# Cross-attention values on four 64 by 64 parts of TensorE, copied out by ScalarE in half partitions

## The chip, the cores and the metric

The kernel runs on one core of one Trainium2 chip. The metric is the device time of one execution in microseconds (us); the time of a kernel is the median of its runs.

## What is computed

One decoder layer over x (16 batches of 64 tokens, 256 wide), in float32: self attention with 16 heads, cross attention with 16 heads over a context of 64 positions per batch, and a mixture of 16 experts with 4 per token plus a shared one. Each is added to x after a layer norm. The change lies in the cross attention:

```python
scores = jnp.einsum('bhsr,bhlr->bhsl', q_r, k_r)
attn = jax.nn.softmax(scores, axis=-1)
ctx_c = jnp.einsum('bhsl,bld->bhsd', attn, kv_r)        # the values: 64 positions l, 64 features d
ctx_lat = jnp.einsum('bhsd,hkd->bhsk', ctx_c, w_kc_kv)
ctx = ctx_lat.transpose(0, 2, 1, 3).reshape(Bv, Sv, H * K)
return ctx @ Wo.T
```

The kernel works in B = 16, S = L = 64 for these. The last two products are folded into one matrix per head before.

## The kernel before, in words

**One order for all engines.** The generators `rounds`, `middle` and `block_order` write out one list of named steps by hand. Each of the five engines walks the whole list and issues its part of each step, so on every engine the work stands in the order of the list. Semaphores alone tie the engines to each other.

**Stages.** Self attention comes first (`rounds`). Then `middle` interleaves the query rotation (`rotate`, 24 steps in two halves g of 12: twelve 128 by 128 matmuls on TensorE, L776, four products with the rope tables on VectorE, L1401, and sums on GpSimd, L1754 and L1757), the scores' left operand (`latents` and `latents_end`, matmuls on the four 64 by 64 parts of the array, L790, copied by ScalarE, L1121), and the cross attention of 8 tiles t of two batches q each. After it the router decides on experts, GpSimd scatters the rows of 8 tiles to a table in memory (`scatter`, 32 indirect transfers, L1782), and 47 blocks of 128 rows go through the experts (`block_order`).

**The cross attention of tile t** has these steps, spread out in `middle` with other work between them:
- `cross_scores`: 32 matmuls of 64 by 64 (L824) into banks 2 and 3 of PSUM. VectorE takes the row maximum off (`less_max`, L1332 and L1334, into `sm`), ScalarE takes the exponential (`cross_exp`, L1127), VectorE sums, inverts and scales (`cross_norm`, L1345, L1347, L1448, each for one head parity at a time).
- `cross_turn`: 8 records of transposes (L834); ScalarE copies them to `PX` (L1136), with partitions 64*odd + l: the head's parity `odd`, and the context position l.
- `cross_values`: for each batch q one matmul of 128 by 128 weights `kv2` by 512 columns of `PX` (L843). `kv2` is block diagonal, with the same 64 by 64 context block for both parities, so half of each product is with zeros. Float32 matmuls stand as two records each in the trace: four records a tile. Each q has a PSUM bank, which ScalarE copies to `CT` (L1144), 128 partitions by 512 elements, one copy per q.
- `cross_out`: 8 matmuls (16 records) of 128 by 256 with `CT` as weights (L852), after both copies. VectorE adds the result to x (L1453), and that frees the layer norm of the tile (`norm`, `center`, `norm_turn` with s = 2).

**What stands between.** On TensorE, between `cross_values(t)` and `cross_out(t)`: two `rotate` steps for t = 0, 1 and 2, `cross_scores(5)` for t = 3, `cross_turn(5)` for t = 4, `cross_scores(7)`, `cross_turn(6)` and a `norm_turn` for t = 5, a `norm_turn` and a `turn_hidden` for t = 6, `hidden(1)` for t = 7. On ScalarE, behind the `CT` copies: `cross_exp(2)` for t = 1; `copies(0)` (L1168) for t = 3; `expert(1)` (L1183), `copies(1)`, `cross_turn(5)`, `cross_exp(6)`, `split2` (L1161) and `split13` (L1157) for t = 4. `split2` and `split13` also have a part on GpSimd (L1765, L1761), which subtracts what ScalarE rounded.

Banks of PSUM are taken from a ring of six in these steps; `take` waits until the bank's last content is drained.

Of the kernel before, what the change touches and what calls it, by code (L numbers as in the profile page):

```python
# [8 lines left out]
ACT = mybir.ActivationFunctionType  # L9
# [298 lines left out]
def b3(t2, c):  # L308
    return t2.rearrange("p (a c) -> p a c", c=c)
# [12 lines left out]
def program(nc, x, codes, scl, woc, wos, bq, bk, bv, bo, tabs, cks, plan, empty, kvc, wqr, wkr, kckv, wot,  # L322
            wqx, kcq, wg, w13, w2, ex, out):
    with ExitStack() as ctx:
# [3 lines left out]
        def at(name, offset, shape, dt=F):  # L328
            return nc.alloc_sbuf_tensor_at(name, shape, dt, offset=offset)
# [3 lines left out]
        def keep(name, shape, dt=F):  # L333
            n = 4
            for d in shape[1:]:
                n *= d
            n = (n + 31) // 32 * 32
            t = at(name, ofs[0], shape, dt)
            ofs[0] += n
            return t  # L340
# [8 lines left out]
        kv2 = keep("kv2", [128, 16, 128])  # L349
# [117 lines left out]
        PX = at("PX", R3 + 36864, [128, 2, 8, 64])  # L467
        CT = at("CT", R3 + 40960, [128, 8, 128])
# [37 lines left out]
        ps = Banks(psum, sem)  # L506
# [72 lines left out]
        def tensor_program():  # L579
            te = Engine(nc.tensor)  # L580
            pe = nc.tensor
            ring = [0, 1, 4, 5]

            def free(b):
                if b >= 6:
                    te.wait_ge(s_x2, 8)
                te.wait_ge(ps.drained[b], ps.turn[b])
                if b in ps.lent:
                    te.wait_ge(*ps.lent.pop(b))

            def take(*name, steps=1):
                b = ring.pop(0)
                ring.append(b)
                free(b)
                return b, ps.place(b, *name, steps=steps)[0]
# [240 lines left out]
                    mm.then_inc(ps.full[b], 1)  # L836

            def cross_values(t):
                for q in range(2):
                    b, ap = take("cv", t, q)  # L840
                    te.wait_ge(*ps.emptied("ct", t, 0))
                    te.wait_ge(*ps.emptied("ct", t, 1))
                    pe.matmul(ap, kv2[:, 2 * t + q, :], PX[:, q, :, :].rearrange("p h s -> p (h s)"),  # L843
                              start=True, stop=True).then_inc(ps.full[b], 1)

            def cross_out(t):
                b, ap = take("co", t)
# [149 lines left out]
            def direct(k):  # L997
                b = NB - DIRECT + k
                ap, free = ps.place(1, "direct", k)
                if k == 0:  # L1000
# [10 lines left out]
                    "query_weights": query_weights, "rotate": rotate, "latents": latents,  # L1011
                    "latents_end": latents_end,
                    "cross_scores": cross_scores, "cross_turn": cross_turn, "cross_values": cross_values,
                    "cross_out": cross_out, "widen": widen, "logits": logits, "hidden": hidden,
                    "turn_hidden": turn_hidden, "down": down, "rank": rank, "table": table,
# [8 lines left out]
        def scalar_program():  # L1024
            sc_ = Engine(nc.scalar)
            act = nc.scalar.activation
# [110 lines left out]
                        ACT.Copy).then_inc(ps.drain("ct", t, n), 1)  # L1137

            def cross_values(t):
                for q in range(2):  # L1140
                    sc_.wait_ge(*ps.filled("cv", t, q))
                    if t > 0:
                        sc_.wait_ge(*ps.filled("co", t - 1))
                    act(CT[:, :, 64 * q:64 * q + 64], b3(ps.of("cv", t, q), 64),  # L1144
                        ACT.Copy).then_inc(ps.drain("cv", t, q), 1)

            def route(n, part):
                if part == 0:
# [68 lines left out]
            def block_down(b):  # L1217
                sc_.wait_ge(*ps.filled("by", b))
                if b >= 4:
# [5 lines left out]
                    "context_turn": context_turn, "query_key_blocks": query_key_blocks, "out_blocks": out_blocks,  # L1225
                    "query_weights": query_weights, "latents_end": latents_end, "cross_exp": cross_exp,
                    "cross_turn": cross_turn, "cross_values": cross_values, "route": route, "split13": split13,
                    "split2": split2, "copies": copies, "expert_in": expert_in, "expert": expert, "hidden": hidden,
                    "turn_hidden": turn_hidden, "block_turn": block_turn, "block_hidden": block_hidden,
# [833 lines left out]
```

## Time and profile before

| | |
|---|---|
| median of 3 runs | 550.94 us (550.25 to 551.01) |
| span of the profiled execution | 542.0 us |
| median less span | 8.9 us |
| TensorE busy | 505.6 us, 93% |
| VectorE busy | 405.6 us, 75% |
| ScalarE busy | 252.4 us, 47% |
| GpSimd busy | 200.2 us, 37% |
| chain that ended last | TensorE 67%, VectorE 18%, DMA 6%, issue 4% |
| `cross_values` on TensorE | 32 records, 288.1 to 388 us |
| `CT` copies on ScalarE | 16, median 592 ns |

Times in the profile are us from the start of the span. Busy shares are averages over stages with different limits. A row of the timeline has start, duration, engine (PE is TensorE, DVE VectorE, ACT ScalarE, POOL GpSimd), line, tile names and shapes, and in square brackets the idle time before it and what ended it. A row of the chain has start, duration and what ran; the chain is followed back from the last instruction of the kernel.

### The profile page before, as it was taken

The numbers are of one execution on the slowest core, as the hardware profiler recorded it, in microseconds if no ns is written. First come the engines' busy times: TensorE is split into PE (matmuls) and PEld (weight loads), VectorE is DVE, ScalarE is ACT, GpSimd is POOL, SyncE is SP. The second block draws the span as 40 slices with busy tenths as digits, with TensorE's granted clock in tenths as the row PEclk, the third lists the DMA queues.
The fourth block names the chain that finished last, engine by engine and source line by source line (L and its number), as shares of the span: only waits on it lengthen the run. The fifth ranks groups of instructions, "written<-read, shape, count | busy, mean of one in ns | idle before, by whom it ended". The sixth has DMA issues, their size and how long they took to land.

```text
span 542.0 us, 12555 instructions
## 1 busy us (share of the span) xinstructions
PE 505.6 (93%) x4841; PEld 412.0 (76%) x4841; DVE 405.6 (75%) x968; ACT 252.4 (47%) x560; POOL 200.2 (37%) x172
## 2 busy tenths in 40 slices
PE   5988999999999999999999999969988799999994
PEld 5767888888878889576567666747878688999993
DVE  6699875636736386999599787898886799657776
ACT  2454746537485564001212331483354687665552
POOL 7855450013100000433255244042867534544440
PEclk9899999999999999999999999997998999999998
DMA  8246100024062039993000000800282683556543
GB/s 291 112 160 197 46 2 1 1 99 186 21 211 93 2 114 372 320 346 131 1 1 2 2 1 5 309 2 14 91 268 96 212 303 99 147 164 180 168 135 118
DMA packets 22299, 68.09 MB, mean 126 GB/s; under 512 B 3979, under 2 KB 12595, under 8 KB 21204
## 3 DMA queue, kind: packets, MB, share of 16 engines
q1 hardware_dynamic: 17180, 54.45, 30.6%
q0 software_dynamic: 3600, 8.43, 4.3%
q10 hardware_dynamic: 1460, 4.40, 2.2%
q8 instruction: 40, 0.66, 0.5%
q14 instruction: 19, 0.16, 0.1%
HBM read 57.79 MB, written 28.48 MB: 159 GB/s over the span
## 4 chain that ended last, share of the span: by engine, by line
PE 67%; DVE 18%; DMA 6%; issue 4%; POOL 2%; ACT 1%; SPq 1%; POOLq 0%; DVEq 0%; ACTq 0%
PE psum L619 11%; PE psum L776 10%; PE psum L699 6%; PE psum L632 5%; PE psum L970 5%; PE psum L790 4%; PE psum L684 4%; PE psum L852 4%; DVE tt L1401 3%; DMA yv<-parts_of_tokens 3%; PE psum L652 2%; PE psum L843 2%; DVE sm L1448 2%; PE psum L661 2%; PE psum L761 2%
## 5 line engine op out<-in xcount | busy, mean ns | idle before, releaser
L1754 POOL TENSOR_TENSOR rp<-tt,tt 128x512 f32<-128x512 f32 x24 | 30.9, 1287 | 134.7 <-DVE tt L1401 134.7
L1401 DVE TENSOR_TENSOR tt<-psum,tab 128x512 f32<-128x512 f32 x96 | 60.1, 680 | 11.7 <-PE psum L776 10.7
L970 PE MATMUL psum<-EW,xgh 128*128 (+1 forms) x188 | 56.5, 343 | 1.2 <-DVE xgl L1617 1.1
L619 PE MATMUL psum<-xTh,W 128*128 128x512 f32 x128 | 52.4, 409 | 2.1 <-DVE W L1299 2.1
L1790 POOL DMA_INDIRECT parts_of_tokens<-yb,xg x35 | 35.4, 1010 | 50.1 <-ACT yb L1221 47.6
L619 PE MATMUL psum<-xTl,W 128*128 128x512 f32 x128 | 51.3, 401 | 0.0
L1363 DVE TENSOR_TENSOR OTl<-psum,OTh 128x256 fp32r<-128x256 f32 (+1 forms) x49 | 23.2, 502 | 26.9 <-ACT OTh L1084 26.8
L776 PE MATMUL psum<-xTh,Ah 128*128 128x512 f32 x96 | 40.1, 418 | 0.0
L1782 POOL DMA_INDIRECT rows_of_experts<-xe,posi x32 | 33.7, 1052 | 14.0 <-issue 8.6
L776 PE MATMUL psum<-xTh,Al 128*128 128x512 f32 x96 | 38.0, 396 | 0.0
L776 PE MATMUL psum<-xTl,Ah 128*128 128x512 f32 x96 | 38.0, 396 | 0.0
L970 PEld LDWEIGHTS psum<-EW,xgh 128*128 128x128 f32 x188 | 34.1, 188 | 2.1 <-issue 1.9
L699 PE MATMUL psum<-wo,OTh 128*128 128x256 f32 x128 | 34.1, 300 | 0.0
L1617 DVE TENSOR_TENSOR xgl<-psum,xgh 128x256 fp32r<-128x256 f32 x47 | 19.7, 422 | 18.5 <-ACT xgh L1203 18.1
L1121 ACT ACTIVATE qP<-psum 128x512 f32<-128x512 f32 x16 | 8.7, 595 | 51.4 <-PE psum L790 51.4
L1696 POOL TENSOR_TENSOR rst<-bst,half 128x1 f32<-128x1 f32 x24 | 13.0, 553 | 50.9 <-DVE bst L1258 50.2
L699 PE MATMUL psum<-wo,OTl 128*128 128x256 f32 x128 | 31.7, 282 | 0.0
L790 PE MATMUL psum<-rp,Mb 64*64 64x512 f32 x256 | 30.8, 599 | 0.8 <-DVE rp L1426 0.6
L1048 ACT ACTIVATE qT<-psum,bqs 128x512 f32<-128x512 f32 x32 | 21.9, 685 | 20.3 <-PE psum L619 20.2
L852 PE MATMUL psum<-Fb,CT 128*128 128x256 f32 x128 | 30.6, 394 | 0.2 <-ACT CT L1144 0.2
L619 PEld LDWEIGHTS psum<-xTh,W 128*128 128x128 f32 x128 | 24.6, 192 | 8.0 <-DVE W L1299 2.3
L970 PE MATMUL psum<-EW,xgl 128*128 (+1 forms) x94 | 30.4, 323 | 0.0
(263 smaller groups left out, 1462.0 us busy)
## 6 DMA issues: line engine op xcount, KB each, us to landing
rows_of_experts<-in_empty SPq DMA_DIRECT2D x8, 2064.0 KB, 24.7
exr<-in_ex SPq DMA_DIRECT2D x9, 608.0 KB, 6.8
xg<-rows_of_experts SPq DMA_DIRECT2D x39, 129.0 KB, 2.2
exr<-in_ex ACTq DMA_DIRECT2D x7, 608.0 KB, 6.3
yv<-parts_of_tokens SPq DMA_DIRECT2D x8, 512.0 KB, 4.3
raw<-in_codes SPq DMA_DIRECT2D x6, 512.0 KB, 6.4
raw<-in_codes SPq DMA_DIRECT2D x3, 1024.0 KB, 8.0
wor<-in_woc SPq DMA_DIRECT2D x4, 512.0 KB, 3.8
```

What stands on the lines that cost most here:

```text
L619: mm = pe.matmul(ap, W[:, kt, m, 512 * hq + 128 * h:512 * hq + 128 * h + 128], xp[:, kt, 512 * g:512 * g + 512], start=(n == 0), stop=(n = ...
L632: mm = pe.matmul(ap, xp[:, kt, 128 * t:128 * t + 128], W[:, kt, 2, 512 * hq:512 * hq + 512], start=(n == 0), stop=(n == 3))
L699: mm = pe.matmul(dst, part[i % 2][:, 128 * h:128 * h + 128], wo[:, 4 * hq + h, :], start=(hq == 0 and h == 0 and n == 0 and i % 2 == 0), s ...
L776: mm = pe.matmul(ap, w[:, kt, half_, 128 * j:128 * j + 128], xp[:, kt, 512 * g:512 * g + 512], start=(n == 0), stop=(n == 5))
L790: mm = pe.matmul(ps.of(*name)[64 * side:64 * side + 64, :], Mb[r, q, side, 2 * half_ + head // 2, :], tiles[i][r, half_, :], start=(first ...
L852: mm = pe.matmul(ap[:, 0:256], CT[:, hp, :], Fb[:, hp, :], start=(hp == 0), stop=(hp == 7))
L970: mm = pe.matmul(ap[:, 0:352], xp[b % 2][:, 128 * kt:128 * kt + 128], piece(b, o + 352 * kt, 352), start=(k == 0), stop=(k == 5))
L1363: op = tt_(by_batch(OTl[i % 2][:, :])[of], src, by_batch(f32(OTh[i % 2][:, :]))[of], ALU.subtract)
L1401: return tt_(b3(tt[n][:, :], 64), b3(src, 64), tab[:, j % 3, n, :].unsqueeze(1).to_broadcast([128, 8, 64]), ALU.mult)
L1754: tt_(o[:, 0, :], tt[0][:, :], tt[1][:, :], ALU.subtract).then_inc(s_rp_lo, 1)
L1782: nc.gpsimd.indirect_dma_start(out=rows_of, out_offset=to, in_=xe[:, t % 4, k, :], in_offset=None, bounds_check=SPARE - 1, oob_is_err=Fals ...
L1790: nc.gpsimd.indirect_dma_start(out=parts_of, out_offset=to, in_=yb[b % 4][:, :], in_offset=None, bounds_check=4 * 1024 - 1, oob_is_err=Fal ...
```

## The change

The values run as four matmuls of 64 by 64 weights by 512 columns, one for each batch q and parity `odd`; the zero blocks of `kv2` are not read any more. A parity's two products go to one bank (batch q to partitions 64q on). TensorE takes both banks ahead of the first matmul. ScalarE copies each bank in two instructions of 64 partitions by 512 elements, as the parity must move to partitions 64*odd of `CT`: four copies a tile where there were two of 128 partitions. Nothing else is touched, and the number of semaphore steps stays.

```diff
             def cross_values(t):
+                parity = [take("cv", t, odd) for odd in range(2)]
+                te.wait_ge(*ps.emptied("ct", t, 0))
+                te.wait_ge(*ps.emptied("ct", t, 1))
                 for q in range(2):
-                    b, ap = take("cv", t, q)
-                    te.wait_ge(*ps.emptied("ct", t, 0))
-                    te.wait_ge(*ps.emptied("ct", t, 1))
-                    pe.matmul(ap, kv2[:, 2 * t + q, :], PX[:, q, :, :].rearrange("p h s -> p (h s)"),
-                              start=True, stop=True).then_inc(ps.full[b], 1)
+                    for odd, (b, ap) in enumerate(parity):
+                        r = slice(64 * odd, 64 * odd + 64)
+                        mm = pe.matmul(ap[64 * q:64 * q + 64, :], kv2[r, 2 * t + q, r],
+                                       PX[r, q, :, :].rearrange("p h s -> p (h s)"), start=True, stop=True)
+                        if q == 1:
+                            mm.then_inc(ps.full[b], 1)
...
             def cross_values(t):
-                for q in range(2):
-                    sc_.wait_ge(*ps.filled("cv", t, q))
+                for odd in range(2):
+                    sc_.wait_ge(*ps.filled("cv", t, odd))
                     if t > 0:
                         sc_.wait_ge(*ps.filled("co", t - 1))
-                    act(CT[:, :, 64 * q:64 * q + 64], b3(ps.of("cv", t, q), 64),
-                        ACT.Copy).then_inc(ps.drain("cv", t, q), 1)
+                    for q in range(2):
+                        op = act(CT[64 * odd:64 * odd + 64, :, 64 * q:64 * q + 64],
+                                 b3(ps.of("cv", t, odd)[64 * q:64 * q + 64, :], 64), ACT.Copy)
+                    op.then_inc(ps.drain("cv", t, odd), 1)
```

## Rows read from the trace of the kernel before

**Rows 1.** The page: its head.

```profile
span 542.0 us, 12555 instructions
```

**Rows 2.** The chain that ended last, 284 to 312 us: start, us, what.

```profile
288.52 1.72 PE psum L843 x4
...
303.13 1.88 PE psum L790 x16
```

**Rows 3.** Groups by shape, ScalarE: busy, mean ns of one, idle before.

```profile
L1078 ACT ACTIVATE PT<-psum 64x256 f32<-64x256 f32 x32 | 12.1, 379 | 0.4
```

**Rows 4.** The timeline of ScalarE: half partitions at 91 us, whole ones at 343 us.

```profile
91.48 0.38 ACT L1078 ACTIVATE PT<-psum 64x256 f32<-64x256 f32 x1
91.89 0.60 ACT L1084 ACTIVATE OTh<-psum 128x512 fp32r<-128x512 f32 x1
...
343.41 1.13 ACT L1144 ACTIVATE CT<-psum 128x512 f32<-128x512 f32 x2
```

**Rows 5.** The timeline of tile 1 on VectorE, TensorE and ScalarE.

```profile
300.89 0.75 DVE L1448 TENSOR_TENSOR sm<-sm,rs 128x512 f32<-128x512 f32 x1
...
302.04 1.09 PE L834 MATMUL psum<-ident,sm 128*128 128x128 f32 x8
...
306.11 0.60 ACT L1144 ACTIVATE CT<-psum 128x512 f32<-128x512 f32 x1
...
307.46 1.14 ACT L1127 ACTIVATE sm<-sm 128x512 f32<-128x512 f32 x2
...
308.11 0.69 DVE L1345 TENSOR_REDUCE sums<-sm 128x8 f32<-128x512 f32 x1 [2.20 <-ACT sm L1127]
```

**Rows 6.** The timeline of tile 2 on TensorE and VectorE.

```profile
319.22 0.95 PE L834 MATMUL psum<-ident,sm 128*128 128x128 f32 x7 [0.18 <-DVE sm L1448]
...
326.92 1.89 DVE L1401 TENSOR_TENSOR tt<-psum,tab 128x512 f32<-128x512 f32 x3 [0.71 <-PE psum L776]
```

**Rows 7.** The timeline of tile 3 on TensorE and VectorE.

```profile
345.31 0.92 PE L852 MATMUL psum<-Fb,CT 128*128 128x256 f32 x3
...
349.07 0.42 DVE L1453 TENSOR_TENSOR xs<-psum,xs 128x256 f32<-128x256 f32 x1 [0.47 <-PE psum L852]
```

**Rows 8.** The timeline of tiles 4 to 6 on four engines.

```profile
353.44 0.58 ACT L1144 ACTIVATE CT<-psum 128x512 f32<-128x512 f32 x1
...
354.23 0.60 ACT L1144 ACTIVATE CT<-psum 128x512 f32<-128x512 f32 x1 [0.20 <-PE psum L843]
...
354.97 3.69 PE L852 MATMUL psum<-Fb,CT 128*128 128x256 f32 x16
...
359.08 0.42 DVE L1453 TENSOR_TENSOR xs<-psum,xs 128x256 f32<-128x256 f32 x1
...
360.25 1.83 POOL L1765 TENSOR_TENSOR w2l<-w2r,w2h 128x768 fp32r<-128x768 f32 x1 [7.83 <-ACT w2h L1161]
...
360.36 2.25 DVE L1448 TENSOR_TENSOR sm<-sm,rs 128x512 f32<-128x512 f32 x1
...
363.49 2.70 DVE L1448 TENSOR_TENSOR sm<-sm,rs 128x512 f32<-128x512 f32 x1
...
366.24 1.97 PE L834 MATMUL psum<-ident,sm 128*128 128x128 f32 x8 [4.77 <-DVE sm L1448]
```

**Rows 9.** Windows of TensorE's line 852, tiles 5 and 6: busy, PEclk the granted clock.

```profile
368.70:373.50 4.80, 4.80 (x16) 3.61 (x15) 0.72 0.00 0
```

**Rows 10.** The timeline of tiles 6 and 7 on ScalarE and TensorE.

```profile
376.77 0.60 ACT L1144 ACTIVATE CT<-psum 128x512 f32<-128x512 f32 x1 [0.54 <-PE psum L843]
...
378.37 3.69 PE L852 MATMUL psum<-Fb,CT 128*128 128x256 f32 x16 [0.23 <-ACT CT L1144]
...
386.69 1.06 ACT L1144 ACTIVATE CT<-psum 128x512 f32<-128x512 f32 x2
...
388.86 3.61 PE L852 MATMUL psum<-Fb,CT 128*128 128x256 f32 x16
```

**Rows 11.** The timeline of GpSimd: first of the 20 scatters that follow each other.

```profile
395.90 1.04 POOL L1782 DMA_INDIRECT rows_of_experts<-xe,posi  x1 [1.44 <-DVE posi L1550]
```

## The prediction, made before the changed kernel was run

> **What bounds the kernel now.** I read the page first, then the chain that ended last through the cross attention (284 to 395 us), then the timeline of each tile there, always asking which wait ended last before `cross_out`. The span is 542.0 us [rows 1]; the median of the runs, 550.94 us, is 8.9 us above it. I take those 8.9 us as unchanged, so a shift of the span is added to the median.
>
> In the chain, the values of a tile stand on TensorE with 1.72 us [rows 2]. So TensorE's time there looks as if it counted. But the timeline shows three engines that take turns: TensorE waits for VectorE ahead of the transposes of tiles 2 and 6 [rows 6, 8], VectorE waits for ScalarE's exponential of tile 2 for 2.20 us [rows 5], and TensorE waits for the `CT` copies ahead of `cross_out(6)` [rows 10]. What the change saves is on TensorE; what it adds is on ScalarE, behind which the others stand. ScalarE's small busy share says nothing of that.
>
> **The price of each part.** *TensorE.* Removed: four records of 128 by 128, 1.72 us a tile [rows 2]. Added: four matmuls on four different parts of the array, eight records. The nearest rows are those of L790, the same shape on the same four parts: 16 records, two rounds of four matmuls, in 1.88 us [rows 2], so one round is 0.94 us. Saved: 0.78 us a tile, 6.2 us over eight. Both banks are now full 0.94 us after the start, where the first was full after 0.86 us; so ScalarE's first copy can begin about 0.1 us later than today, if ScalarE is free.
>
> *ScalarE.* Removed: two copies of 128 partitions, 1.13 us from the start of the first to the end of the second [rows 4]; one takes 0.60 us, the second starts while the first ends. Added: four copies of 64 partitions by 512 elements. No such copy is in the trace. One instruction should last as long as today, as it goes by the elements in a partition: a half-partition copy of 256 elements takes 379 ns [rows 3], just as long as whole-partition ones of that size. The question is the overlap. In the 32 pairs of half-partition copies, the second begins only when the first is done (0.4 us of idle time over 32, 0.01 each [rows 3]), and what comes next, 0.03 us after its end [rows 4]. Bounds: starts 0.49 us apart with the overlap (0.60 less some 0.11, from the 1.13 us of a pair [rows 4]), 0.61 us apart without it. I take 0.61, as its rows are the ones on half partitions. Four copies then end 3 x 0.61 + 0.59 = 2.42 us after the first start, and the next instruction starts 0.02 us later. The other end gives 3 x 0.49 + 0.59 = 2.06 us. Two of the four also move data to the other half of the partitions; no row shows that. As an upper bound I allow 0.1 us more for each copy.
>
> The Trainium skill (ScalarE: Activation LUTs, What ACT_TABLE_LOAD costs) says that back-to-back ACTIVATEs overlap by about 93 ns, and makes no exception for half partitions. By that rule the sum would be the small one below; the rows on half partitions speak against it. The skill's TensorEngine Tiling (Array Packing), PSUM Bottleneck, warns of this very trade: tiling speeds up TensorE but not the evacuation of PSUM, and the access should be joined over tiles in a bank, which the change takes apart.
>
> *Waits and banks.* The second bank is taken 0.86 us earlier. The step that waits today at the ring of banks, `cross_values(4)`, waits for its first bank; I cost this at nothing. DMA, VectorE and GpSimd issue what they issued before.
>
> **The sum, tile by tile** (how much later than today, along the path that counts).
> - Tile 0: TensorE is 0.78 us early. The transposes of tile 1 start at 302.04 us, but VectorE has their input ready only at 300.89 + 0.75 = 301.64 us [rows 5]. Of the gain 0.3 us is left: -0.3.
> - Tile 1: ScalarE starts on `CT` at 306.11 us today, just as it comes free [rows 5]; now at 305.81. `cross_exp(2)`, queued behind it, starts 2.44 us later, at 308.25 instead of 307.46 us. VectorE waits for it (2.20 us idle today [rows 5]), and the delay goes through its products for the rotation to the transposes of tile 2, which already wait for VectorE [rows 6]: +0.79. TensorE's own gain is lost in that wait.
> - Tile 2: TensorE saves 0.78. Behind it two rotations cover the copies (5.6 us against 2.42), and `cross_exp(3)` is wanted late. VectorE waits for TensorE in those rotations [rows 6], so the gain passes on: 0.0.
> - Tile 3: copies start at 343.41 us [rows 4], as ScalarE comes free, and end at 345.83 us. TensorE has one short step of cover, `cross_scores(5)`, and began `cross_out(3)` at 345.31 us [rows 7]. It needs 0.14 us after the copies: 345.97 us. VectorE already waits for this product [rows 7]: +0.66.
> - Tile 4: the first copy starts at 353.44 + 0.66 = 354.10 us and the last ends at 356.52 us; `cross_out(4)` starts at 356.66 us instead of 354.97 [rows 8], 1.69 us late, and ends at 360.35 us. VectorE would have come to its sum at 359.08 + 0.66 = 359.74 us [rows 8], so it waits until 360.38 us: +1.30.
> - Then VectorE's L1448 meets GpSimd's L1765, as today. L1448 normally lasts 0.7 us; it lasts 2.25 us while GpSimd splits `w2`, and 2.70 us while it splits `w13` [rows 8]. Both come later by the same copies: GpSimd starts some 5.1 us after the copies' end (today 360.25 less 354.83, less 0.4 us in which ScalarE waits for an exponential's input), at 361.6 us; VectorE at 360.36 + 1.30 = 361.66 us. So GpSimd is ahead by 0.1 us, as it is today, and nothing changes but the time: +1.30.
> - Tile 5: TensorE idles for 4.77 us before the transposes of tile 6 [rows 8], which hides both its gain and the copies.
> - Tile 6: TensorE comes early, and has only short transposes as cover. Copies from 376.77 + 0.1 to 379.29 us, `cross_out(6)` at 379.43 instead of 378.37 us [rows 10]: +1.06, total +2.36.
> - Tile 7: copies from 386.69 to 389.11 us, `cross_out(7)` at 389.25 instead of 388.86 us [rows 10]: +0.39, total +2.75. `hidden(1)` covers the rest.
> - After that the rank of tiles 3 to 5 follows `cross_out(7)` on TensorE, and 20 scatters follow it without a pause from 395.90 us [rows 11]. I see no slack there: the 2.75 us reach the end.
>
> 550.94 + 2.75 = **553.7 us**, 0.5% slower. A difference of 0.2% (1.1 us) is about what a measurement of this kernel can tell from none.
>
> **Rivals.**
> 1. *The copies overlap* (starts 0.49 us apart, next start 1.96 us after the first). Tile 1 gives +0.31, tile 2 -0.47, tile 3 -0.17, tile 4 +0.1, tile 6 +0.8, tile 7 nothing: +0.8 us, 551.7 us, no change. For it: all whole-partition copies do this [rows 4]. Against: the 32 pairs [rows 3]. Chance 0.20.
> 2. *The meeting at 361 us turns round* and the kernel is faster. If VectorE's L1448 starts before GpSimd's L1765, it is over in 0.7 us (362.35 us). GpSimd's first split then ends at about 364.1 us, VectorE's second L1448 is let in there and is done by 364.7 us, where my forecast has 366.19 + 1.30 = 367.49 us [rows 8]: 2.8 us less. TensorE then idles for half as long. Today it comes out of the idle time at 0.72 of the full clock over `cross_out(5)`, partly at 1.2 GHz, which took 4.8 us [rows 9] and takes 3.6 us at 2.4 GHz [rows 10]; up to 1.3 us may come back. Result 2.75 - 2.8 - 1.3, so about 549.6 us. It decides at a shift of the two by 0.1 us against each other. For: today's distance is as small (360.25 and 360.36 us [rows 8]). Against: both hang on the same copies. Chance 0.15. The Trainium skill (SBUF — State Buffer, SBUF: two separate sides) calls this an exclusive lock that goes to whichever starts first for its whole instruction; by that rule the order decides all, and the two long L1448 agree with it.
> 3. *TensorE is all that counts*: 6.2 us saved, 544.7 us. For it stands the chain [rows 2]. Against: the waits for VectorE and `CT` [rows 6, 8, 10]. Chance 0.04.
> 4. *The copies that cross partitions are dearer*, or a new wait for a bank adds to it: 0.1 us a copy is 0.4 us at each of tiles 1, 3, 4, 6 and 7, 2.0 us: 555.7 us. Chance 0.06.
>
> My forecast keeps 0.55. Range: from 549.3 (most of rival 2) to 555.3 us. Faster by over 0.2%: 0.17 (rivals 2 and 3, less the case that the clock gives nothing back). Within 0.2%: 0.22. Slower: 0.61.
>
> **What would show it.** Right: L843 with 64 records, a tile's start to the next step in 0.9 to 1.0 us; 32 copies at L1144 of 64 by 512 of about 0.59 us with starts 0.61 apart; a wait of TensorE for `CT` at tiles 3, 4, 6 and 7, none at 0, 1, 2; VectorE's wait for the exponential of tile 2 about 1 us longer; L1448 still 2 to 3 us long at 361 to 367 us; `cross_out(7)` 2 to 3 us later. Wrong: starts 0.49 us apart (rival 1); a first L1448 of 0.7 us with L1765 behind it (rival 2); `cross_out(7)` earlier than 388 us with no wait for `CT` (rival 3).

## The result, and the profile after

| | before | with the change |
|---|---|---|
| median of 15 runs each, same chip | 551.14 us (548.66 to 557.52) | 558.13 us (551.23 to 564.74) |
| ratio, with 95% interval | | 1.0106 [1.0081, 1.0132] |
| TensorE busy | 505.6 us | 507.6 us |
| ScalarE busy | 252.4 us | 262.9 us |

The change makes the kernel slower by 5.8 us (4.5 to 7.3 us; 1.06% of 551.14 us). The forecast was 553.7 us, 2.75 us slower, in a range of 549.3 to 555.3. Its sign was right, and so was most of its path. Its size was not: the measured loss is over twice as large, and the sum lacked a mechanism, TensorE's clock, as the last sections show. TensorE is busy for 2.0 us more, though its values take 0.9 us less in each of eight tiles: a first sign that its other work took longer. Medians here and below are over all runs, while the ratios leave out the disturbed ones, so the two can differ.

The page of the changed kernel, its head:

```profile
span 557.9 us, 12639 instructions
```

This execution took 559.19 us, so only 1.3 us lie outside its span; in every other run on record it is 1.3 to 1.5 us. [rows 1] and the median of before had 8.9 us between them, and I had read that as work outside the span. It was not: the execution that I read must have been about 8 us shorter than the median. More on that below.

The `CT` copies of the changed kernel, grouped by shape (durations are minimum, median and maximum in ns), with what TensorE waited for:

```profile
L1149 ACT ACTIVATE CT<-psum x32: 574/592/596, 291.2 to 391.5; 64x512 f32<-64x512 f32 x32
...
  PE psum L856: 4.8, 3
```

A copy of half the partitions takes 592 ns, as long as a whole one did, and there are twice as many. TensorE (L856 is `cross_out`) waits 4.8 us for them in three places; before, the one such wait on the path was 0.23 us [rows 10].

The timeline of the changed kernel, in order of time, at tiles 1, 2, 3, 5, 6 and 7 (cut where dots stand):

```profile
305.16 1.04 PE L845 MATMUL psum<-PX,kv 64*64 64x512 f32 x8
306.40 2.41 ACT L1149 ACTIVATE CT<-psum 64x512 f32<-64x512 f32 x4
306.66 0.47 PE L776 MATMUL psum<-xTh,Ah 128*128 128x512 f32 x1 [0.46 <-ACT qP L1125]
308.83 1.15 ACT L1131 ACTIVATE sm<-sm 128x512 f32<-128x512 f32 x2
309.50 0.69 DVE L1351 TENSOR_REDUCE sums<-sm 128x8 f32<-128x512 f32 x1 [3.26 <-ACT sm L1131]
...
324.84 0.47 PE L776 MATMUL psum<-xTh,Ah 128*128 128x512 f32 x1 [0.46 <-ACT qP L1125]
...
343.02 1.09 PE L845 MATMUL psum<-PX,kv 64*64 64x512 f32 x8
343.99 1.16 PE L824 MATMUL psum<-kv,qP 64*64 64x64 f32 x64
346.95 3.69 PE L856 MATMUL psum<-Fb,CT 128*128 128x256 f32 x16 [1.80 <-ACT CT L1149]
...
362.60 1.81 POOL L1771 TENSOR_TENSOR w2l<-w2r,w2h 128x768 fp32r<-128x768 f32 x1 [8.56 <-ACT w2h L1167]
362.62 2.34 DVE L1454 TENSOR_TENSOR sm<-sm,rs 128x512 f32<-128x512 f32 x1
...
365.83 2.70 DVE L1454 TENSOR_TENSOR sm<-sm,rs 128x512 f32<-128x512 f32 x1
...
377.64 1.09 PE L845 MATMUL psum<-PX,kv 64*64 64x512 f32 x8
...
381.33 3.69 PE L856 MATMUL psum<-Fb,CT 128*128 128x256 f32 x16 [1.88 <-ACT CT L1149]
...
389.53 0.53 PE L884 MATMUL psum<-w13h,xTh 128*128 128x352 f32 x1 [0.30 <-DVE ex_lb L1485]
389.66 2.40 ACT L1149 ACTIVATE CT<-psum 64x512 f32<-64x512 f32 x4
389.86 0.50 PE L884 MATMUL psum<-w13l,xTh 128*128 128x352 f32 x1
...
393.08 3.64 PE L856 MATMUL psum<-Fb,CT 128*128 128x256 f32 x16
```

Read it against the steps of the prediction.

- Tile 1: four copies last 2.41 us together, so their starts are 0.61 us apart ((2.41 - 0.59) / 3). The exponential starts 0.02 us after their end, and VectorE waits for it 3.26 us where it waited 2.20 [rows 5].
- Tiles 3, 4 and 6: TensorE stands 1.80, 1.13 and 1.88 us for `CT`. At tile 6 that was 0.23 us [rows 10]; at tile 3 `cross_out` had begun without a wait [rows 7].
- Tile 7: the forecast wait for `CT` is not there. The copies end at 392.06 us (389.66 + 2.40), and `cross_out(7)` starts only at 393.08 us, right behind `hidden(1)`.
- Tile 5: VectorE and GpSimd meet as before: 2.34 and 2.70 us for the two L1454 beside 2.25 and 2.70 us of [rows 8]. The order didn't turn round.
- Two things in this timeline were not forecast. The rotation behind `cross_values` of tiles 1 and 2 waits 0.46 us for a bank that ScalarE has to empty (`qP`). And behind tile 7 the matmuls of `hidden(1)` take 0.50 us each.

The second of these is the clock. The same stretch (`hidden(1)`) in both kernels, as windows: width, busy time and count of TensorE, weight loads, VectorE, ScalarE and GpSimd, the granted TensorE clock, the DMA share and GB/s. First before:

```profile
387.00:390.50 3.50, 3.50 (x21) 3.32 (x20) 3.19 (x27) 2.34 (x5) 3.01 (x4) 1.00 0.30 109
```

And with the change:

```profile
389.80:393.00 3.20, 3.20 (x12) 3.20 (x12) 2.86 (x22) 2.53 (x5) 2.19 (x3) 0.50 0.22 80
```

The granted clock is 1.00 (2.4 GHz) before and 0.50 (1.2 GHz) after. Before, the same matmul took this long (timeline of TensorE):

```profile
387.09 0.32 PE L880 MATMUL psum<-w13l,xTh 128*128 128x352 f32 x1
```

What TensorE did before the clock fell: a wait of 1.88 us for `CT` (till 381.33), `cross_out`, transposes, 18 router matmuls of only 16 columns (385.9 to 388.1 us), then the values in 1.09 us where the kernel before spent 1.96 us on wide ones, and an idle time of 0.30 us.

### The profile page after: what moved, and what is told of

It is laid out like the page before. It is cut to its first block, busy times and chain, and to the rows that moved or that the text cites. A ratio compares the mean times of both kernels' runs of the same rounds, so it can differ in the third digit from the quotient of the medians.

```text
span 557.9 us, 12639 instructions
## 1 busy us (share of the span) xinstructions
PE 507.6 (91%) x4873; PEld 415.3 (74%) x4873; DVE 405.7 (73%) x968; ACT 262.9 (47%) x576; POOL 199.2 (36%) x172
## 4 chain that ended last, share of the span: by engine, by line
PE 62%; DVE 23%; issue 5%; ACT 4%; DMA 3%; POOL 1%; another core or an unknown queue 1%; SPq 0%; ACTq 0%; DVEq 0%; POOLq 0%
PE psum L619 11%; PE psum L776 7%; PE psum L699 6%; PE psum L632 5%; DVE tt L1407 4%; PE psum L856 4%; PE psum L790 4%; PE psum L684 4%; PE psum L974 3%; DVE EW L1594 3%; PE psum L884 3%; PE psum L652 2%; DVE sm L1454 2%; DMA yv<-parts_of_tokens 2%; ACT CT L1149 2%
## 5 line engine op out<-in xcount | busy, mean ns | idle before, releaser
L974 PEld LDWEIGHTS psum<-EW,xgh 128*128 128x128 f32 x188 | 34.6, 191 | 2.9 <-issue 2.7
L856 PE MATMUL psum<-Fb,CT 128*128 128x256 f32 x128 | 30.1, 390 | 4.8 <-ACT CT L1149 4.8
L856 PEld LDWEIGHTS psum<-Fb,CT 128*128 128x128 f32 x128 | 24.9, 198 | 8.8 <-issue 5.3
```

Of the source, the lines that this page charges most:

```text
L856: mm = pe.matmul(ap[:, 0:256], CT[:, hp, :], Fb[:, hp, :], start=(hp == 0), stop=(hp == 7))
L974: mm = pe.matmul(ap[:, 0:352], xp[b % 2][:, 128 * kt:128 * kt + 128], piece(b, o + 352 * kt, 352), start=(k == 0), stop=(k == 5))
```

## The experiments

A ratio below is against runs of the kernel before on the same chip. A line number in an experiment is that of its own kernel. I also compare traces by milestones: the start of the transposes or of `cross_out` of a tile, counted from the start of the transposes of tile 0. That takes out how early or late the cross attention began as a whole.

**1. Both kernels once more.** The first pair of traces could not say what belongs to the change and what to one execution.

> The kernel before, unchanged, for a second trace. The first trace has a span of 542.0 us, and the runs have a median of 551 us, so the first trace may be of an unusually short execution. Theory A (the shift of the changed kernel reaches the end one to one; the rest is how executions differ): span of 546 to 552 us, cross_out(7) at 388 to 390 us, and the stretch from there to the end 5 to 9 us longer than in the first trace. Theory B (both traces are typical, and the delay grows after cross_out(7)): span within 2 us of 542.

> The changed kernel again, for a second trace. Both theories: cross_out(7) 3.5 to 4.5 us later than before, copies 0.60 us apart. Theory A: from cross_out(7) to the end as long as in the second trace of before, within the 3 us by which executions differ, and the waits of 9.3 us on ScalarE and 4.1 us on VectorE near 410 us are gone or elsewhere. Theory B: those waits stand there again.

> The kernel before, a third trace, to see which stretches of low granted clock belong to it. Theory C (the change brings low clock by letting TensorE wait): no stretch of granted clock 0.5 between 330 and 360 us nor between 385 and 400 us; cross_out(7) 103.8 to 104.3 us after the transposes of tile 0, as in the first two traces. Theory D: such a stretch is there too.

> The changed kernel, a third trace. Theory C: a stretch of granted clock 0.5 near 390 us, and in some executions one near 344 us; cross_out(7) 108 us after the transposes of tile 0, or 110 where both are there. Theory D: the position changes freely from trace to trace, and there may be none.

These executions took 559.0 and 559.53 us (before) and 555.2 and 555.17 us (the change): the slower kernel had the shorter ones. The medians of the kernel before on these chips are 553.07 and 553.47 us, so both its traces are of long executions, as the first was of a short one. So one execution doesn't tell the size of the change. Inside the cross attention the traces agree much better. Milestones in us, three traces of each:

| start of | before | change | shift of the means | forecast |
|---|---|---|---|---|
| transposes 2 | 34.6, 34.6, 34.6 | 35.5, 35.5, 35.5 | +0.9 | +0.79 |
| transposes 3 | 53.2, 53.2, 53.2 | 53.8, 53.8, 53.8 | +0.6 | 0.0 |
| `cross_out(3)` | 60.7, 61.3, 60.7 | 61.9, 61.9, 62.4 | +1.2 | +0.66 |
| transposes 4 | 64.2, 64.8, 64.3 | 65.4, 67.4, 66.0 | +1.8 | +0.66 |
| `cross_out(4)` | 70.3, 70.9, 70.4 | 72.5, 74.6, 73.1 | +2.9 | +1.69 |
| `cross_out(6)` | 93.7, 93.2, 93.6 | 96.3, 98.4, 97.2 | +3.8 | +2.36 |
| `cross_out(7)` | 104.2, 103.7, 104.1 | 108.0, 110.1, 108.6 | +4.9 | +2.75 |

The 4.9 us lie within the measured 4.5 to 7.3 us. The spread between executions comes later. From the start of `cross_out(7)` to the end the kernel before takes 153.1, 169.1 and 171.7 us in its three traces, the changed one 164.8, 158.9 and 162.2. The waits between 395 and 440 us show where (engine, what waited, for what: us in total, times, longest). The second trace of before:

```profile
ACT sl L1190 <- remote: 7.9, 1, 7.9
...
DVE xs L1613 <- remote: 3.8, 1, 3.8
```

The first trace of the change:

```profile
ACT sl L1196 <- remote: 9.3, 1, 9.3
```

And the trace on which the prediction rests has no wait of that kind. Its longest on that line is 3.3 us:

```profile
ACT sl L1190 <- PE psum L880: 9.7, 10, 3.3
```

"remote" means that nothing the trace shows released it. I don't know what it is. It comes in both kernels, and in every trace of this document but the one that I read: 7.9 to 9.3 us on ScalarE each time. So theory A is wrong where it had that wait gone from the second trace of the change, and the tail of the second trace of before is 16 us longer than the first, not 5 to 9. It is right in that the wait doesn't come from the change.

TensorE's granted clock goes with the length of this tail. The window of 400 to 440 us, in the first and in the third trace of before:

```profile
400.00:440.00 40.00, 32.60 (x221) 30.33 (x220) 30.32 (x108) 22.19 (x42) 24.20 (x21) 0.96 0.60 207
400.00:440.00 40.00, 22.32 (x121) 21.18 (x120) 21.89 (x70) 8.89 (x19) 20.13 (x18) 0.74 0.32 104
```

The clock there is 0.96, 0.79 and 0.74 in the three traces of before and 0.83, 0.91 and 0.87 in those of the change. In the order of that clock, from 0.96 down, the tails behind `cross_out(7)` take 153.1, 158.9, 162.2, 164.8, 169.1 and 171.7 us. TensorE also idles more where the clock is lower, so this doesn't show which of the two brings the other.

The traces of the change also say more on the clock. It is 0.50 near 390 us in all three, and in two of three also at tile 3: from 344 to 351 us in the second, over `cross_scores(5)` and `cross_out(3)`, and from 341 to 345 us in the third, ahead of `cross_out(3)`. A window of the second trace of the change:

```profile
344.00:350.00 6.00, 4.84 (x72) 4.05 (x67) 5.21 (x10) 4.81 (x8) 0.00 (x0) 0.51 0.98 348
```

Its timeline of TensorE at tile 3, to be set beside the 1.16 and 3.69 us above:

```profile
343.80 1.80 PE L824 MATMUL psum<-kv,qP 64*64 64x64 f32 x64
346.77 5.51 PE L856 MATMUL psum<-Fb,CT 128*128 128x256 f32 x15 [1.16 <-ACT CT L1149]
```

In none of the three traces of before is the clock below 1.00 at either place.

**2. ScalarE's half alone.** TensorE computes the values as before; each bank, which now holds both parities of one batch, is copied in two halves. `CT` gets what it got before.

```diff
-                    act(CT[:, :, 64 * q:64 * q + 64], b3(ps.of("cv", t, q), 64),
-                        ACT.Copy).then_inc(ps.drain("cv", t, q), 1)
+                    for odd in range(2):
+                        r = slice(64 * odd, 64 * odd + 64)
+                        op = act(CT[r, :, 64 * q:64 * q + 64], b3(ps.of("cv", t, q)[r, :], 64), ACT.Copy)
+                    op.then_inc(ps.drain("cv", t, q), 1)
```

> TensorE as before; each bank is copied in two half-partition copies, four a tile. My account (half-partition copies do not overlap and stand in the path at tiles 1, 3, 4, 6 and 7): copies 0.60 to 0.61 us apart; cross_out(7) 5 to 7 us later than before, as TensorE's savings are missing too; time 1.2 to 2% over before. Rival (copies are off the path, and the change lost its time to TensorE's 64 by 64 parts): within 0.3% of before.

Measured: 558.13 us against 553.07, ratio 1.0083 [1.0048, 1.0118]. The timeline of ScalarE at tile 1:

```profile
304.19 2.42 ACT L1146 ACTIVATE CT<-psum 64x512 f32<-64x512 f32 x4
306.63 1.15 ACT L1127 ACTIVATE sm<-sm 128x512 f32<-128x512 f32 x2
```

The copies last as long here, where none of them crosses partitions, as in the change (2.41 us). So the crossing costs nothing, and the half partitions alone cost the time. `cross_out(7)` starts 4.3 us later than before (108.3 against a mean of 104.0): less than the 5 to 7 us expected, as is the time, 0.8% for 1.2 to 2%. The window over `hidden(1)` shows the clock whole:

```profile
388.00:391.00 3.00, 2.75 (x15) 2.03 (x13) 2.66 (x20) 2.63 (x6) 2.49 (x4) 1.00 0.24 88
```

**3. TensorE's half alone.** The matmuls of the change, but ScalarE copies each bank whole. Half of the values then land in other places of `CT`, so the output is another; the amount of work is right.

```diff
-                    for q in range(2):
-                        op = act(CT[64 * odd:64 * odd + 64, :, 64 * q:64 * q + 64],
-                                 b3(ps.of("cv", t, odd)[64 * q:64 * q + 64, :], 64), ACT.Copy)
-                    op.then_inc(ps.drain("cv", t, odd), 1)
+                    act(CT[:, :, 64 * odd:64 * odd + 64], b3(ps.of("cv", t, odd), 64),
+                        ACT.Copy).then_inc(ps.drain("cv", t, odd), 1)
```

> TensorE as in the change (four parts, a bank per parity), but each bank copied whole, two copies of 128 partitions a tile. The values then land in other places of CT than the reference's, so later numbers differ; the work is the same. My account: ScalarE as before, TensorE 0.78 us less a tile, of which tiles 2, 3, 6 and 7 pass some on, but VectorE sets the start at tiles 1, 2 and 6: 2 to 4 us faster than before (0.4 to 0.7%). Rival (TensorE is all that counts): 6 us faster, 1.1%. Rival (the 64 by 64 parts cost something in themselves): not faster than before.

Measured: 552.50 us against 553.07, ratio 0.9983 [0.9941, 1.0026]. `cross_out(7)` starts 2.6 us earlier than before (101.4). The time itself shows no gain clear of its interval; 0.4 to 0.7% was expected. The timeline of ScalarE at tile 1:

```profile
304.93 1.09 ACT L1148 ACTIVATE CT<-psum 128x512 f32<-128x512 f32 x2
305.88 1.17 ACT L1131 ACTIVATE sm<-sm 128x512 f32<-128x512 f32 x2
```

Two whole copies take 1.09 us and the next instruction starts 0.95 us after the first: they overlap with what follows by 0.14 us, which the half ones never do. Together, 2 and 3 show that the copies alone bring a loss and that TensorE's own part is a gain up to `cross_out(7)`. They also show that TensorE's gain alone is some 2.6 us of the 6.2 that its busy time promises. The two shifts add to +1.6 us, while the change itself has +4.9. By the sum put right below, some 1.7 us of these are the low clock, which neither half has; the other 3.2 us are only 1.1 less than the copies alone cost, so over half of TensorE's gain is lost beside the longer copies.

**4. The change at some tiles alone.** First at tiles 0, 2 and 5, where the prediction found the copies covered; then at the other five. The lines for TensorE; ScalarE's step is chosen in the same way:

```diff
+            def cross_values(t):
+                (values_new if t in (0, 2, 5) else values_old)(t)
```

> The change at tiles 0, 2 and 5 alone, where other TensorE work covers the copies; tiles 1, 3, 4, 6 and 7 as before. My account by tile: cross_out(7) 0.4 to 1.1 us earlier than before against the transposes of tile 0, within 0.2% or 0.3% of before. Rival (each tile costs the same): half of the change's loss, 0.4% slower.

> The change at tiles 1, 3, 4, 6 and 7 alone, where the copies stand in the path; tiles 0, 2 and 5 as before. My account by tile: transposes of tile 2 about 1.1 us late, cross_out(3) 1.7, cross_out(4) 2.8, cross_out(6) 3.4, cross_out(7) 3.8 us late against the transposes of tile 0, plus 0.9 us or more where the granted clock falls near 390 us; 0.8 to 1.3% slower than before. Rival (each tile costs the same): five eighths of the change's loss.

Measured: at 0, 2, 5 a ratio of 1.0036 [1.0006, 1.0066]; at 1, 3, 4, 6, 7 a ratio of 1.0076 [1.0030, 1.0121]. By the trace `cross_out(7)` starts 0.9 us earlier in the first (103.2) and 6.5 us later in the second (110.5), with the clock low near 342 and 390 us; expected were 3.8 us and 0.9 more for the clock near 390, with nothing for the clock near 342. So the exposed tiles carry the loss, as the prediction had it. But in the first kernel trace and time contradict each other: 0.9 us earlier up to `cross_out(7)`, some 2 us later at the end. Its ten runs spread from 550.27 to 561.98 us; I can't say more on it.

**5. Idle time filled.** If TensorE's idle time at tiles 3, 4 and 6 lowers its clock, matmuls in that time should keep the clock up. Four matmuls of 128 by 128 by 256 columns whose result nobody reads go into the bank of `cross_out`, ahead of it:

```diff
+                te.wait_ge(*ps.emptied("fb", 3))
+                for _ in range(4 if t in (3, 4, 6) else 0):
+                    pe.matmul(ap[:, 0:256], Fb[:, 0, 0:128], Fb[:, 0, :], start=True, stop=True)
```

> The change, plus four matmuls of 128 by 128 by 256 into cross_out's bank ahead of its wait for CT at tiles 3, 4 and 6 (overwritten by the first real one), so that TensorE works where it idled for 1.2 to 1.9 us. Theory C (part of the loss is the TensorE clock: low granted clock at 344 us in one trace of the change and near 390 us in both, none there in the two traces of before): no stretch of granted clock 0.5 between 330 and 360 us nor between 385 and 400 us; cross_out(7) 2.8 to 3.2 us later than before against the transposes of tile 0 instead of 3.7 and 5.8; 0.2 to 0.5% faster than the change. Theory D (the clock has other causes): the low stretches stay, and the time is that of the change or more.

> The change with four filler matmuls at tiles 3, 4 and 6 again, beside the unfilled one on the same chip. Theory C: no stretch of granted clock 0.5 between 330 and 360 us nor between 385 and 400 us, cross_out(7) 107.0 to 107.8 us after the transposes of tile 0. Theory D: such a stretch appears.

Measured: a ratio of 1.0111 [1.0057, 1.0165], no gain against the change's 1.0106, where 0.2 to 0.5% was expected; the single run of the repeat took 562.16 us. In the first trace the clock is whole at both places:

```profile
341.00:345.00 4.00, 4.00 (x85) 3.02 (x85) 3.83 (x9) 3.21 (x6) 0.00 (x0) 1.00 0.99 367
388.00:391.00 3.00, 2.40 (x16) 1.92 (x12) 2.69 (x21) 2.48 (x5) 1.99 (x3) 1.00 0.13 48
```

The timeline of TensorE there shows the fillers (L854) in the place of the wait:

```profile
343.58 1.99 PE L854 MATMUL psum<-Fb 128*128 128x256 f32 x8
345.45 3.69 PE L859 MATMUL psum<-Fb,CT 128*128 128x256 f32 x16
```

In the repeat the clock was whole near 342 us, but 0.50 near 390. A third kernel has the fillers and also issues the four matmuls of `cross_values(7)` twice, which gives TensorE back the 0.9 us of 512-column matmuls right ahead of `hidden(1)`:

```diff
-                for q in range(2):
+                for n, q in enumerate((0, 1, 0, 1) if t == 7 else (0, 1)):
```

> The change with the fillers of tiles 3, 4 and 6, and the two rounds of cross_values(7) issued twice, so that TensorE works 1.9 us there, about as long as before; the banks are full 0.9 us later, of which ScalarE is busy otherwise for 0.5 us. Theory C: no stretch of granted clock 0.5 between 330 and 360 us nor between 385 and 400 us; hidden(1) takes 2.3 us again and cross_out(7) stands 107.2 to 108.0 us after the transposes of tile 0. Theory D: the low stretch near 390 us is there again, and cross_out(7) at 108.5 us or later.

Measured, in four runs: a ratio of 1.0169 [1.0058, 1.0280]. Its timeline of TensorE:

```profile
389.76 1.95 PE L845 MATMUL psum<-PX,kv 64*64 64x512 f32 x16
391.64 0.42 PE L887 MATMUL psum<-w13h,xTh 128*128 128x352 f32 x1
391.90 0.32 PE L887 MATMUL psum<-w13l,xTh 128*128 128x352 f32 x1
...
394.42 1.75 PE L859 MATMUL psum<-Fb,CT 128*128 128x256 f32 x7 [0.57 <-ACT CT L1152]
```

And its windows, with the clock at tile 3 (low in spite of the fillers) and over `hidden(1)` (whole); `cross_out(7)` starts at 109.7 us, where 107.2 to 108.0 were expected:

```profile
344.00:347.00 3.00, 3.00 (x61) 2.61 (x52) 2.86 (x7) 2.93 (x6) 0.00 (x0) 0.50 0.96 322
391.60:393.90 2.30, 2.24 (x16) 1.92 (x12) 2.02 (x18) 2.00 (x4) 1.61 (x2) 1.00 0.16 57
```

What follows. Over the kernels with the change at tiles 3, 6 and 7 and no filler (five traces: three of the change, the exposed tiles, and experiment 6 below) the clock is low near 390 us in all and near 342 us in four. With fillers (three traces) it is low near 390 us in one and near 342 us in one. In the three traces of before, and with only one half of the change, or whole copies (experiments 2, 3 and 7), or the change at covered tiles alone (six traces), it is never low at either place. So the low clock near 390 us belongs to the change at these tiles. That speaks for the theory that saved matmul time and waits together lower it, but five traces against three with fillers don't settle that. The fillers bring no time that the measurement shows. In the traces `cross_out(4)` starts 0.5 us later with them than in the first trace of the change (73.0 against 72.5), and `cross_out(7)` at 107.6 and 108.1 us beside 108.0 to 110.1: they cost some of what the clock gives back.

**6. The banks turned.** The rotation behind `cross_values` takes the next banks of the ring, which ScalarE is still emptying. Here the ring is turned by two banks behind the values of tiles 1 and 2, so that the rotation finds the ones that are free the longest.

```diff
+                if t in (1, 2):
+                    ring[:4] = ring[2:4] + ring[:2]
```

> The change, with the ring of banks turned by two behind the values of tiles 1 and 2, so that the rotation after them takes the two banks of the transposes, drained 2 us before, and not those of the qP copies. Theory E (the bank cost tile 2 its gain): no idle time of TensorE between L845 and L776 at tiles 1 and 2; transposes of tile 3 at 53.3 to 53.5 us after those of tile 0, where the change has 53.8 and before 53.3; cross_out(3) 0.3 to 0.5 us earlier than in the change; too little for the time to show. Rival (the rotation is set by VectorE anyway): transposes of tile 3 stay at 53.8 us.

Measured, in four runs: a ratio of 1.0124 [1.0033, 1.0214]. The timeline of TensorE at tile 1:

```profile
304.01 1.04 PE L845 MATMUL psum<-PX,kv 64*64 64x512 f32 x8
304.98 0.50 PE L776 MATMUL psum<-xTh,Ah 128*128 128x512 f32 x1
```

The wait of 0.46 us is gone, and the transposes of tile 3 start at 53.3 instead of 53.8 us: 0.5 of the 0.6 us by which the milestones had missed the forecast. At tile 3 the gain is lost again in this trace (`cross_out(3)` at 62.0 against 61.9 us): the stretch ahead of it, 341 to 345 us, is at the low clock.

**7. A layout that lets the copies stay whole.** The half copies are needed because a bank of the change holds one parity of both batches. If `cross_scores` puts the odd heads of batch 1 where the even ones were, and the even where the odd were, the values can be computed on four parts and each bank still holds both parities of one batch, in the right partitions. Softmax, transposes and copies don't care which head is which. What the layer computes stays the same.

```diff
 def cross_scores(t):
-                            mm = pe.matmul(sides[odd][0][64 * q:64 * q + 64, 64 * hp:64 * hp + 64],
+                            side = odd ^ q
+                            mm = pe.matmul(sides[side][0][64 * q:64 * q + 64, 64 * hp:64 * hp + 64],
...
-                                mm.then_inc(ps.full[2 + odd], 1)
+                                mm.then_inc(ps.full[2 + side], 1)
 def cross_values(t):
...
+                for q, (b, ap) in enumerate(banks):
+                    for odd in range(2):
+                        r = slice(64 * (odd ^ q), 64 * (odd ^ q) + 64)
+                        mm = pe.matmul(ap[64 * odd:64 * odd + 64, :], kv2[r, 2 * t + q, r],
+                                       PX[r, q, :, :].rearrange("p h s -> p (h s)"), start=True, stop=True)
+                    mm.then_inc(ps.full[b], 1)
```

> A version that keeps the reference's result and both halves of the gain. cross_scores puts batch q = 1 of a parity into the other parity's bank, so the transposed probabilities of q = 1 stand with the parities' partitions exchanged; the values of q = 1 then run on the two off-diagonal 64 by 64 parts and land on the partitions where CT wants them. TensorE takes 0.94 us a tile for the values, as in the change; ScalarE keeps two copies of 128 partitions. My account: as pe_only, cross_out(7) 2 to 3 us earlier than before against the transposes of tile 0, 0.3 to 0.5% faster than before. Rival (TensorE's parts do not run at once if two row parts write one bank): L843's eight records take 1.7 us or more, no gain.

> The version with exchanged parities for q = 1 again, to narrow its interval: cross_out(7) 101.4 to 101.8 us after the transposes of tile 0, 2.2 to 2.9 us earlier than before; 0.3 to 0.6% faster than before.

> The version with exchanged parities for q = 1, with the same turn of the ring. Theory E: transposes of tile 3 at 51.9 to 52.1 us after those of tile 0 instead of 52.4, cross_out(7) at 101.1 to 101.3 us instead of 101.5; 0.4 to 0.7% faster than before. Rival: as swap, 0.3 to 0.5%.

Measured: ratios of 0.9951 [0.9911, 0.9991] and 0.9972 [0.9937, 1.0006]; with the turned ring 0.9987 [0.9938, 1.0035]. The timeline at tile 1, TensorE and ScalarE:

```profile
303.94 1.04 PE L846 MATMUL psum<-PX,kv 64*64 64x512 f32 x8
305.18 1.09 ACT L1148 ACTIVATE CT<-psum 128x512 f32<-128x512 f32 x2
```

The matmuls are as short as in the change and the copies as short as before. `cross_out(7)` starts 2.5 and 2.6 us earlier than before in the two traces (101.6 and 101.4), and 3.0 us earlier with the turned ring (101.0). Against the changed kernel that is over 7 us. Against the kernel before the first measurement is a gain by its interval, the repeat only just not, and the turned ring's 0.5 us more is too small to be seen in the time. Of the kernels here the exchanged layout is the one to keep.

## Why the prediction was wrong in size, point by point

- **"I take 0.61, as its rows are the ones on half partitions": right.** Four copies in 2.41 us, forecast 2.42; next start 0.02 us later. The other bound, 0.49, does not follow from the 1.13 us of a pair, which gives 0.53; it is what pairs of 1.06 [rows 10] and 1.09 us give. Rival 1, by which they overlap, is refuted by the starts 0.61 us apart here and in experiment 2. The Trainium skill (ScalarE: Activation LUTs, What ACT_TABLE_LOAD costs) says that back-to-back ACTIVATEs overlap by about 93 ns: here that holds for whole-partition copies (0.14 us in experiment 3) and not for half ones. The Trainium skill (TensorEngine Tiling (Array Packing), PSUM Bottleneck) warns that tiling speeds up TensorE but not the emptying of PSUM: here that even became longer, 2.41 us of copies for 1.09.
- **One round in 0.94 us: right.** The four matmuls (eight records) last 1.04 us from the first start to the last end, and in experiment 6, where no wait hides it, the next step starts 0.97 us after the first.
- **Crossing partitions (rival 4): nothing.** Experiment 2 has the same times without it. The other half of rival 4, a new wait for a bank, did come, as told below.
- **Tile 0, -0.3: too large.** The transposes of tile 1 start 17.3 us behind those of tile 0 instead of 17.4, so only 0.1 us of the gain was left.
- **Tile 1, +0.79: right** within 0.1 us, 0.9 us measured, as less gain came in from tile 0.
- **"Waits and banks ... I cost this at nothing", and from it "Tile 2 ... the gain passes on: 0.0": wrong by 0.5 us.** This is the first step that failed. Both banks are now taken at once and TensorE arrives 0.8 us earlier, at banks that ScalarE's `qP` copies don't empty before. 0.46 us of the gain is spent in that wait, as experiment 6 shows by taking it away.
- **Tiles 3, 4 and 6: the waits for `CT` came where the sum had them.** The sum took 0.66 us for tile 3; from the transposes of tile 3 to `cross_out(3)` the means differ by 0.6 us (8.3 against 7.7). At tile 7 the wait did not come in the first trace of the change: the slow `hidden(1)` took its place. The meeting of VectorE and GpSimd kept its order, so rival 2 didn't come. The Trainium skill (SBUF — State Buffer, SBUF: two separate sides) calls the port that the two share an exclusive lock, and the 2.34 and 2.70 us agree: each L1454 ends about 0.55 us after GpSimd's instruction beside it. Rival 3 is refuted by the waits.
- **A term that is missing: TensorE's clock.** This is the second step that failed, and the larger one. I used the clock only for rival 2, as something that could be given back. The sum took every matmul of the changed kernel at 2.4 GHz. From `cross_out(6)` to `cross_out(7)` the kernel before takes 10.5 us in each trace; the change takes 11.8, 11.6 and 11.5 at the low clock; experiments 2 and 5 (first trace), with the same copies at the whole clock, take 10.9. So the copies cost the forecast 0.4 us there, and the low clock 0.8 us more. The first trace says so too: its copies were done 1.0 us before `cross_out(7)` began, where in experiment 2, at the whole clock, 0.15 us lie between. From the transposes of tile 3 to those of tile 4 the change takes 11.6 us with the whole clock and 13.7 and 12.2 us with the low one: 2.1 and 0.6 us, 0.9 on the mean of three traces.
- **The sum put right:** 2.75 + 0.1 (tile 0) + 0.5 (bank) + 0.8 (clock near 390) + 0.9 (clock near 345) = 5.05 us, against +4.9 at `cross_out(7)` and 5.8 [4.5, 7.3] measured. That the clock was low there is shown. That TensorE's saved work and its waits brought it down is supported, not shown.
- **"8.9 us above it. I take those 8.9 us as unchanged": wrong as a reading**, though it cancels in a difference. Only 1.3 us lie outside the span. The rest was one short execution, without the unnamed wait of 7.9 to 9.3 us that every later trace has behind 400 us, and with a higher clock there. The cause is open.
- **"I see no slack there: the 2.75 us reach the end": neither shown nor refuted.** Executions of one kernel differ behind `cross_out(7)` by up to 19 us, which hides it; the clock in that stretch, on which the sum also had no term, goes with the difference.

## What to carry to other kernels

Here a ScalarE copy over half the partitions took as long as a whole one (592 ns for 512 elements in a partition) and lost the overlap with its neighbour too. Before you split a product over parts of TensorE, look for a layout, often one step upstream, in which the banks can still be drained whole. A saving on an engine that then waits is no saving, and on TensorE it may cost its clock as well; count the time in which a faster TensorE will idle. And take two or three traces of the kernel before as the base, compared by milestones near the change, before you read single microseconds out of one.

## What the runs showed that I had not expected

- Two matmuls from different row parts of the array, writing to different partition halves of one bank at the same time (experiment 7), take no longer than into separate banks: 1.04 us for the round of four.
- The granted clock at one place differs between executions of the same kernel: at tile 3 of the change 1.00 in one trace and 0.50 in two.
- ScalarE stands 7.9 to 9.3 us, VectorE up to 5.5 us, behind 400 us for something that the trace doesn't name, in both kernels, yet not in the one execution read first.
- Of six executions of the two kernels, the one with the higher mean clock between 400 and 440 us always has the shorter tail behind `cross_out(7)`: 153.1 us at 0.96, 171.7 us at 0.74.
